# Residual rows stored early, and the second layer's rows added to them in memory by accumulating DMAs

## The reference, cut to what matters

```python
x = x + attn(cond(x, ids_a, ...), ...)            # 8 sequences x 128 rows x 512, float32
x = x + ffn(cond2(x, ids_b, ...), ...)            # the last line: residual + second branch

def ffn(v):                                       # the second branch's end
    h = layernorm(v) * gamma + beta
    h = fake_quant(h) @ fake_quant(w1).T + b1
    h = gelu(h)
    return fake_quant(h) @ fake_quant(w3).T + b3
```

## Time and profile before

| | |
|---|---|
| median of 3 runs | 540.36 us (539.82 to 542.74) |
| the profiled execution, its own time | 543.61 us |
| span of the profiled execution (first to last instruction) | 541.1 us |
| the stage after the loop, about | 490 to 541.1 us of the span |
| the last DMA of the kernel | a store of 256 KB, 2.0 us from issue to landing |

### The profile page before, as it was taken

One profiled execution on the slowest core, in us unless ns is written; L12 is line 12 of the kernel. 1 busy time (PEld: TensorE's weight loads), 2 busy tenths in 40 slices (PEclk: granted clock), 3 DMA queues, 4 the chain that ended last, 5 costly groups with the idle time before them and its releaser, 6 DMA issues.

```text
span 541.1 us, 10845 instructions
## 1 busy us (share of the span) xinstructions
PE 520.7 (96%) x3182; PEld 333.6 (62%) x3182; DVE 475.0 (88%) x630; ACT 428.6 (79%) x1097; POOL 383.6 (71%) x400
## 2 busy tenths in 40 slices
PE   7999999999999999999999999999999999987985
PEld 6754466666666666666666667666666666653442
DVE  4885989998999899989998999899989998966897
ACT  2475578889888888898888887988798878867795
POOL 3004497799789878987998789879977998731063
PEclk9999999999999999999999999999999999999899
DMA  8944137633863385337632763276425642410003
GB/s 276 250 92 121 40 99 207 144 64 91 214 141 68 88 213 136 77 79 212 137 88 79 200 151 85 74 194 155 96 62 152 155 98 58 99 39 1 1 21 136
DMA packets 41341, 63.47 MB, mean 117 GB/s; under 512 B 12452, under 2 KB 20804, under 8 KB 41316
## 3 DMA queue, kind: packets, MB, share of 16 engines
q1 hardware_dynamic: 35652, 46.94, 32.8%
q0 software_dynamic: 3648, 12.75, 11.6%
q10 hardware_dynamic: 2016, 3.48, 2.1%
HBM read 28.55 MB, written 2.10 MB: 57 GB/s over the span
## 4 chain that ended last, share of the span: by engine, by line
PE 82%; DVE 9%; ACT 4%; issue 2%; DMA 2%; POOL 1%; ACTq 0%; SPq 0%; DVEq 0%; POOLq 0%
PE pair L1596 22%; PE pair L1597 22%; PE flow L1719 10%; PE flow L1585 10%; PE flow L1709 5%; PE pair L1497 2%; DVE raw_q L1255 2%; PE pair L1519 2%; PE flow L1497 1%; PE pair L1730 1%; DVE y_max L1373 1%; DVE probs L1385 1%; ACT probs L782 1%; DVE rope_c L1385 1%; DMA stage<-in_x 1%
## 5 line engine op out<-in xcount | busy, mean ns | idle before, releaser
L1271 DVE SCALAR_TENSOR_TENSOR accT<-pair,so_now,accT 128x1024 f32<-128x1024 f32 x103 | 131.7, 1279 | 17.3 <-PE pair L1597 12.3
L1255 DVE SCALAR_TENSOR_TENSOR raw_q<-pair,sc_now,raw_q 128x1024 f32<-128x1024 f32 x90 | 115.2, 1280 | 1.5
L572 POOL TENSOR_TENSOR rope_s<-swap_q,consts 128x512 f32<-128x512 f32 x62 | 85.4, 1378 | 27.6 <-DMA swap_q<-raw_q 27.6
L1596 PE MATMUL pair<-ctx_hi,wo 128*128 128x512 f16 x256 | 97.0, 379 | 4.2 <-ACT wo L757 1.6
L1597 PE MATMUL pair<-ctx_lo,wo 128*128 128x512 f16 x256 | 97.0, 379 | 0.0
L782 ACT ACTIVATE probs<-flow,negmax 128x128 f32<-128x128 f32 x248 | 87.5, 374 | 6.9 <-DVE negmax L1219 6.9
L1596 PE MATMUL pair<-h_hi,wq 128*128 128x512 f16 x240 | 91.0, 379 | 0.0
L1597 PE MATMUL pair<-h_lo,wq 128*128 128x512 f16 x240 | 91.0, 379 | 0.0
L584 POOL TENSOR_TENSOR qT<-rope_c,rope_s 128x512 f32<-128x512 f32 x62 | 85.5, 1380 | 4.7
L572 POOL TENSOR_TENSOR rope_c<-raw_q,consts 128x512 f32<-128x512 f32 x62 | 77.7, 1277 | 1.8 <-DVE raw_q L1255 1.3
L1719 PEld LDWEIGHTS flow<-probsT,v_now 128*128 128x128 f32 x512 | 64.8, 191 | 13.3 <-ACT probsT L842 7.0
(11 more groups left out here) (284 smaller groups left out, 983.7 us busy)
## 6 DMA issues: line engine op xcount, KB each, us to landing
swap_q<-raw_q SPq DMA_DIRECT2D x62, 256.0 KB, 3.7
accT<-part_out POOLq DMA_DIRECT2D x22, 512.0 KB, 4.9
wq_i<-in_L_attn_qw_q SPq DMA_DIRECT2D x8, 1024.0 KB, 5.5
wo_i<-in_L_attn_qw_o SPq DMA_DIRECT2D x32, 256.0 KB, 3.2
swap_k<-raw_k SPq DMA_DIRECT2D x14, 256.0 KB, 3.6
wkv_i<-in_L_attn_qw_k SPq DMA_DIRECT2D x8, 256.0 KB, 5.2
wkv_i<-in_L_attn_qw_v SPq DMA_DIRECT2D x8, 256.0 KB, 5.5
stage<-in_x ACTq DMA_DIRECT2D x4, 256.0 KB, 5.8
```

Source lines behind the costliest of these rows:

```text
L572: pool.tensor_tensor(per_seq(into[:, f, :]), per_seq(source[:, f, :]), on_each_seq(table), ALU.mult).then_inc(done, 1)
L1255: dve.scalar_tensor_tensor(out=into, in0=flat(pair[pair_of(h, (kind, j), last, first)][:, :, :]), scalar=sc_now[:, scale_slot(kind, h), j: ...
L1271: dve.scalar_tensor_tensor(out=a, in0=flat(pair[pair_of(h, (O, c), last, first)][:, :, :]), scalar=so_now[:, (h if c == 0 else h - 1) % 2, ...
L1596: pe.matmul(into[:, f, :], w, upper[:, half[f]], start=True, stop=False)
```

## The change

Two semaphore sets change: one semaphore `d_res[b]` for each of the eight residual stores is new, `out_made` and `out_late` go. SP now waits for `res_kept` and stores `resid[b]` itself to the output. The additions of POOL and DVE go. `scale_product(1, b)` writes straight into `y_out[b]`, of which there are eight, so its wait for `out_made` goes. In POOL's list each `add_residual(b)` for b of 0 and 1 becomes `add_to_output(b)`, and blocks 2 to 7 follow at the end: POOL waits until the store of the residual has landed and the product is scaled, and issues an accumulating DMA from `y_out[b]` onto the output rows in memory.

```diff
@@ SyncE
             for b in range(B):
-                if b < LATE_OUT:
-                    sp.wait_ge(out_made, b + 1)
-                else:
-                    sp.wait_ge(out_late, b - LATE_OUT + 1)
-                sp.dma_start(out[LOW_ORDER[b], :, :], y_out[b]).then_inc(d_out[b % 2], 16)
+                sp.wait_ge(res_kept, b + 1)
+                sp.dma_start(out[LOW_ORDER[b], :, :], resid[b]).then_inc(d_res[b], 16)
             for s in d_out:
                 sp.wait_ge(s, 16 * (B // 2))
@@ GpSimd
-            def add_residual(b):
+            def add_to_output(b):
+                pool.wait_ge(d_res[b], 16)
                 pool.wait_ge(ff_scaled[1], b + 1)
-                pool.wait_ge(res_kept, b + 1)
-                pool.tensor_tensor(y_out[b], probs[:, 0, b % 2, :], resid[b], ALU.add).then_inc(out_made, 1)
+                pool.dma_start(out[LOW_ORDER[b], :, :], y_out[b], accum_op=ALU.add).then_inc(d_out[b % 2], 16)
...
-            add_residual(0)
+            add_to_output(0)
             add_bias(5)
-            add_residual(1)
+            add_to_output(1)
             add_bias(6)
             add_bias(7)
-            add_residual(2)
-            add_residual(3)
+            for b in range(2, B):
+                add_to_output(b)
@@ VectorE
                 dve.wait_ge(ff_done[m], b + 1)
-                if m and 2 <= b < LATE_OUT + 2:
-                    dve.wait_ge(out_made, b - 1)
...
-                out = probs[:, 0, b % 2, :] if m else y_h[:, b % 2, :]
+                out = y_out[b] if m else y_h[:, b % 2, :]
...
-            def add_residual(b):
-                dve.wait_ge(ff_scaled[1], b + 1)
-                dve.wait_ge(res_kept, b + 1)
-                dve.tensor_tensor(y_out[b], probs[:, 0, b % 2, :], resid[b], ALU.add).then_inc(out_late, 1)
...
             scale_product(1, 4)
-            add_residual(4)
             scale_product(1, 5)
-            add_residual(5)
             scale_product(1, 6)
-            add_residual(6)
             scale_product(1, 7)
-            add_residual(7)
```

More of the change, by code:

```diff
@@ L192, in build @@
         d_out = [sem("d_out0"), sem("d_out1")]
+        d_res = [sem(f"d_res{b}") for b in range(B)]
         consts_made, dve_own = sem("consts_made"), sem("dve_own")
@@ L241, in build @@
         stats_done, half_made = sem("stats_done"), sem("half_made")
-        out_made, out_late = sem("out_made"), sem("out_late")
         Q, K, V, O, VALUES = "q", "k", "v", "o", "values"
@@ L338, in build @@
         RESID = [banks[3], banks[7]] + [banks[4]] * (B - 2)
-        LATE_OUT = 4
         def turned_rows(m, b):
```

## The result

The changed kernel takes 544.39 us against 540.61 (medians of 18 runs each beside one another): ratio 1.0069, 95% interval 1.0051 to 1.0087, so 3.7 us slower and over the 0.5% line.

A forecast was written before the change was run, and what follows sets the result against it. After the loop DVE was taken as the bound from 530, ACT beside it from 515. The change gains 1.46 on DVE and gives back 2.5 on DMA: 540.36 + 1.06 = 541.4 us, range 539.2 to 548.6.

The forecast's parts named there:

- likeliest case: Stage after the loop: each accumulating DMA under 1.78 us, time within 0.5% of before, forecast 541.4; chance 0.54.
- DVE, forecast -1.46: End of DVE's list: without four additions, PE is next and DVE's end moves from 538.61 to 537.15, 1.46 us gained.
- SP's early stores at no cost: Eight residual stores issued from 504.0 to 520.27, landed by 522.6, before they are needed; POOL's wait for them costs nothing.
- POOL's issue in place of its addition: POOL's list: a DMA issue costs about 0.9 us against 1.27 for the addition; slowing of later bias additions costed at nothing.
- T = 1.5: Time of one 256 KB accumulating DMA on the DMA engines, in us; 0.9 and 2.7 kept as bounds.
- from 1.78 on: DMA time T in us from which the six at the end would make the kernel over 0.5% (2.7 us) slower.
- The upper bound, 2.7: Longest T, that of the loop's 512 KB accumulating DMA, if the count of rows decides; span then 549.4.
- The rival "two reads for each byte": Accumulating DMAs read addend and target, T = 1.8, twice a store's 0.90; time 543.2, to 548.6 at T = 2.7; chance 0.33.
- The queue of six: Accumulating DMAs of blocks 2 to 7 run one after another without a gap from 532.3 to 541.3, 1.5 each.
- The end, taken over at 0.46: Program's end: the span ends 0.46 us after the last DMA's landing, as after the last store before.
- a DMA wait of SP: Sign that the forecast is right: the chain of waits ends in SP waiting for a DMA, not in DVE.
- 542.16: Forecast end of the changed kernel's span at T = 1.5, against 541.1 before: 1.06 us longer.

The follow-up runs named there:

- the two profiles of the changed kernel: The changed kernel profiled twice, the second time on the chip of a later run: time ratios 1.0069 and 1.0072 to the kernel before.
- the first experiment: Changed kernel with the products stored by SP as plain stores, nothing added (output lacks the residual): ratio 0.9987 to the kernel before.
- the fifth experiment: Changed kernel with only blocks 0 to 3 added by DMA, blocks 4 to 7 by DVE and stored by SP: ratio 1.0017 to the kernel before.
- the second and sixth experiment: Second: changed kernel with POOL's DMAs as plain copies, ratio 1.0013; sixth: block 7 alone added by DMA, others by POOL and DVE, 1.0062; both to the kernel before.
- The fourth experiment: Changed kernel with its accumulating DMAs adding onto the residual's tile in SBUF instead of the output in memory: ratio 1.0056 to the kernel before.
- third experiment: Changed kernel with each accumulating DMA adding half of each row, 256 of 512 columns in 128 rows: ratio 1.0027 to the kernel before.

## Why the prediction was right and where its likeliest case was not

- **DVE, forecast -1.46: right.** -1.37 and -1.49 in the two profiles of the changed kernel, and -1.37 in the first experiment, where the stage keeps -1.33 of it. Between profiles with the same distance ahead of block 2's copy it is 1.49 (30.75 to 29.26, the longer one) and 1.47 (30.85 to 29.38, the shorter one).
- **SP's early stores at no cost: right.** They lie between 503.99 and 519.7, POOL's waits end with DVE's products and never with a store, and the fifth experiment has four of them in a stage of the old length. (The prediction's 522.6 for the last landing should be 522.3 by its own terms, 520.27 and 2.0; nothing hangs on it.)
- **POOL's issue in place of its addition: right in size** (0.85 to 0.91, one of 1.07, and the bias addition behind one runs 1.57 again), **but a term was missing:** from the product to the issue the sum had 0.05 to 0.1, and 0.5 was measured, in the changed kernel and in the second and sixth experiment alike.
- **T = 1.5: too small.** It measured 1.97 and 1.80, and this term alone carries the sum across the 0.5% line (from 1.78 on). The fourth experiment takes the step from the loop's DMA apart. The halving alone misses 0.17: 1.52 is the price in SBUF with rows of 2 KB, against 1.35. With 2.70 for twice the bytes, that puts 0.34 on a part that does not shrink with them, near the 0.4 to 0.6 of the third experiment. Memory as the target adds 0.28 to 0.45, where the forecast had added 0.15 in all. The upper bound, 2.7, held. The rival "two reads for each byte" named 1.8 from twice the store's 0.90, and memory as the target took 2.0 to 2.2 times a copy, SBUF 1.7 times. The Trainium skill's rule beside it ("Collectives: The Full Stack", section "The bandwidth ceiling: the fold count and why AG ≠ RS ≠ AR"), two source reads and so half of a copy's rate, which the page tells of a collective's reduce-scatter, thus fits memory as the target and is too high for SBUF. That reading twice is the mechanism is not shown; the runs show the ratio alone.
- **The queue of six: right in the profiles.** It began 24.4 after block 2's copy, as in the forecast (532.3 there), the engines were busy without a gap, and six took 11.85, six times the 1.95 of the first one alone. That a queue of six is what costs the time is less sure, by the times of the sixth experiment.
- **The end, taken over at 0.46: wrong.** 1.85 was measured. The prediction put the adding DMA in the store's place and kept the store's tail; it did not look at the drain that stands at the end of each queue. In seven profiles with a DMA issued by POOL in the stage, POOL's drain ends 1.3 to 1.7 after the last of its DMAs has landed, by whatever time that was, also for plain copies; where those land early (fifth experiment) it costs nothing. That it waits for them is read from these times; no run took the drain away. The sign that the prediction gave for the chain's end, a DMA wait of SP, therefore did not come: the chain ends in POOL's queue.

So the forecast's sum, mended term by term: 542.16 with the end at 1.85 in place of 0.46 is 543.55, which is 2.45 over 541.1 and just under the 2.7 of the 0.5% line; six times the 0.30 to 0.47 that T was short of are 1.8 to 2.8 more, 4.3 to 5.3 in all, and the two profiles have 4.3 and 5.2. This is the sum of the two profiles; the timed runs give 3.7 and 3.9. The missing half microsecond at the issue doesn't enter, since the first of the six waits for a bias addition and the engines are full from there on. In the prediction's own reckoning T had to reach 1.78 to cost 0.5%; with the true end it would have been 1.54, and the forecast stood at 1.5: the two cases were not as far apart as their times said. That the range held is in part luck: its upper end, 548.6, was the price of T = 2.7 alone, and no term of it stood for a longer end.

## What to carry to other kernels

Additions by DMA that landed ahead of the last stores left the stage as long as before (fifth experiment). As the last work of the kernel such an addition is dear: there its whole latency and the drain of the engine that issued it stand on the path, and 256 KB added onto memory took twice the time of a plain store. Before moving work from an engine to DMAs, count how many of them are issued inside the last few microseconds and multiply by the time of one; if that is longer than the stretch, the DMA engines may be the new bound. And what an engine at the end saves is worth only what the next stores let through: two results ready together still leave one after the other.

## What the runs showed of the hardware that was not expected

- POOL's drain at the program's end ended 1.3 to 1.7 us after the landing of the last DMA that POOL had issued, and 2.6 to 2.7 after its last addition where it had issued none in the stage; with only SP's DMAs last, the span ended 0.4 to 0.5 after the landing.
- From the product that releases it, a DMA on POOL began 0.5 to 0.6 us later; a store on SP, where SP was free, 0.02 to 0.08.
- 256 KB in 128 rows moved in 0.9 us as a copy, in 1.52 when added onto SBUF, in 1.8 to 2.0 when added onto memory in a queue (some 1.9 to 2.3 alone); half of the bytes in as many rows in 1.18.
- TensorE's clock was at 1.2 GHz for some microseconds near the start of this stage in some executions and not in others, of the same kernel too (the changed one without it in the first profile and with it in the second), worth about 1.0 us.
